# Holding GpSimd's scatter of the normalised rows until the last token tile of the second shared pass is reloaded

## The reference

```python
# first sublayer: x1 = x + tanh(g_xattn) * scan_block(ctx, layernorm(x))
# second sublayer: out = x1 + tanh(g_ffn) * ffn(layernorm(x1))
x = hidden_states.reshape(-1, H)                       # 2048 x 512
scores = softmax(einsum('th,eh->te', x, gate_w))
topk_w, topk_idx = top_k(scores, 2)
combine = sum(one_hot(topk_idx, 16) * topk_w[..., None], axis=1)
gu = einsum('th,ehj->etj', x, w_gate_up)               # 16 x 2048 x 704
h = swiglu(gu, 352)
y = einsum('eti,eih,te->th', h, w_down, combine)
y = y + swiglu(x @ shared_gate_up, 704) @ shared_down
```

## Time and profile before

| | us |
|---|---|
| median of 3 runs | 1187.91 |
| lowest and highest | 1187.38, 1188.02 |
| span of the profiled execution | 1213.6 |
| TensorE matmul busy | 990.7 (82%) |
| VectorE busy | 831.8 (69%) |
| ScalarE busy | 560.9 (46%) |
| GpSimd busy | 538.4 (44%) |

### The profile page before, as it was taken

One profiled execution on the slowest core, in us unless ns is written; L12 is line 12 of the kernel. 1 busy time (PEld: TensorE's weight loads), 2 busy tenths in 40 slices (PEclk: granted clock), 3 DMA queues, 4 the chain that ended last, 5 costly groups with the idle time before them and its releaser, 6 DMA issues.

```text
span 1213.6 us, 21853 instructions
## 1 busy us (share of the span) xinstructions
PE 990.7 (82%) x4756; PEld 720.0 (59%) x4765; DVE 831.8 (69%) x1185; ACT 560.9 (46%) x946; POOL 538.4 (44%) x466
## 2 busy tenths in 40 slices
PE   4568977699778897799779998289999999984687
PEld 2144434444344443455479997278898889883576
DVE  4579899898998989999954446154454545444457
ACT  1485875458655685588232122033443544442211
POOL 0056656466555665599611003702433444441164
PEclk9669999899899999999989999689999999996689
DMA  2314111041012300311031013724556665654367
GB/s 76 120 38 174 36 27 50 21 173 36 25 45 89 111 27 26 106 42 46 18 106 43 35 53 111 272 94 138 178 193 212 214 227 203 204 198 135 106 208 233
DMA packets 66229, 134.93 MB, mean 111 GB/s; under 512 B 9344, under 2 KB 13952, under 8 KB 66176
## 3 DMA queue, kind: packets, MB, share of 16 engines
q1 hardware_dynamic: 56496, 103.64, 26.2%
q0 software_dynamic: 8960, 29.37, 6.8%
q10 hardware_dynamic: 720, 1.31, 0.4%
HBM read 161.43 MB, written 42.07 MB: 168 GB/s over the span
## 4 chain that ended last, share of the span: by engine, by line
PE 52%; DVE 21%; issue 15%; ACT 4%; another core or an unknown queue 3%; DVEq 2%; SPq 1%; POOL 1%; ACTq 0%; DMA 0%; POOLq 0%
PE psY L821 12%; PE psG L785 11%; PE psU L785 10%; PE y_ps L689 6%; DVE hst L1280 6%; PE dbu_ps L676 5%; PE psT L778 3%; DVE by_parity L1232 2%; PE psHT L799 2%; DVE sp_t L1266 2%; ACT dA L994 2%; PE mp L643 1%; DVE y L1263 1%; DVE by_parity L1228 1%
## 5 line engine op out<-in xcount | busy, mean ns | idle before, releaser
L509 POOL TENSOR_TENSOR prod<-hst,cbc 128x512 f32<-128x512 f32 x256 | 343.1, 1351 | 249.5 <-DVE hst L1280 242.1
L1280 DVE TENSOR_TENSOR_SCAN hst<-dA,dbu_ps 128x512 f32<-128x512 f32 x256 | 304.8, 1207 | 29.5 <-PE dbu_ps L676 17.9
L689 PE MATMUL y_ps<-prod,ident 128*128 128x512 f32 x512 | 270.0, 610 | 0.9 <-issue 0.4
L676 PEld LDWEIGHTS dbu_ps<-ident,dbuT 128*128 128x128 f32 x1024 | 123.6, 146 | 225.0 <-DVE hst L1280 161.7
L994 ACT ACTIVATE dA<-by_parity,Aneg 128x512 f32 (+1 forms) x256 | 177.6, 715 | 165.6 <-DVE hst L1280 137.8
L676 PE MATMUL dbu_ps<-ident,dbuT 128*128 128x128 f32 x1024 | 166.7, 287 | 74.0 <-DVE hst L1280 69.4
L1094 ACT CAST hh<-psHT 128x384 fp32r<-128x384 f32 x79 | 37.7, 478 | 318.4 <-PE psHT L799 278.8
L821 PE MATMUL psY<-weights,hh 128*128 (+3 forms) x420 | 138.7, 412 | 32.1 <-DVE hl L1475 24.0
L785 PE MATMUL psG<-weights,xh 128*128 (+1 forms) x560 | 141.2, 335 | 14.5 <-issue 9.9
L785 PE MATMUL psU<-weights,xh 128*128 (+2 forms) x560 | 143.0, 337 | 3.7 <-issue 3.7
L1005 ACT ACTIVATE dbuT<-by_parity,BT 128x512 f32 (+1 forms) x192 | 123.7, 707 | 3.3 <-PE dbu_ps L676 3.3
(11 more groups left out here) (176 smaller groups left out, 1358.5 us busy)
## 6 DMA issues: line engine op xcount, KB each, us to landing
raw_gu<-in_L_ffn_w_gate_up_dram SPq DMA_DIRECT2D x100, 704.0 KB
raw_d<-in_L_ffn_w_down_dram SPq DMA_DIRECT2D x50, 512.0 KB
cbc<-c_rows SPq DMA_DIRECT2D x64, 256.0 KB, 3.2
slot_in<-ztile SPq DMA_DIRECT2D x3, 4096.0 KB, 13.7
gbuf<-slot_in SPq DMA_DIRECT2D x48, 256.0 KB, 3.1
slot_out<-yout POOLq DMA_DIRECT2D x48, 256.0 KB, 3.3
raw_d<-in_L_ffn_w_down_dram SPq DMA_DIRECT2D x50, 192.0 KB
xn_rows<-xin SPq DMA_DIRECT2D x16, 256.0 KB, 2.0
```

The lines of the kernel that those rows point to most:

```text
L509: pool.tensor_tensor(prod[:, slot_of(n, j), :], hst[:, slot_of(n, j), :], cbc[:, n % 2, :], ALU.mult).then_inc(prod_ready, 1)
L676: last = tr(dbu_ps[j % 2][:, t * P:(t + 1) * P], dbuT[:, n % 2, t, j * P:(j + 1) * P], ident[:])
L689: mm(y_ps[j][:], ident[:], prod[:, slot_of(n, j), :], start=False, stop=False).then_inc(prod_used, 1)
L1280: V.tensor_tensor_scan(hst[:, slot_of(n, j), :], dA[:, slot_of(n, j), :], dbu_ps[j % 2][:], 0.0, ALU.mult, ALU.add).then_inc(scanned, 1)
```

## The change

One more wait stands on GpSimd's queue ahead of the first indirect DMA of the scatter. Its count is 16 * (8 // 2) = 64, that is the fourth landing in xin's odd buffer since the pass began: tiles 1, 3, 5 and 7. No other instruction is added, removed or moved.

```diff
@@ -541,6 +541,7 @@
             pool.wait_ge(xn_kept, NT)
             pool.wait_ge(pos_ready, 1)
             pool.wait_ge(zeroed, 16 * (NB - 1))
+            pool.wait_ge(xin_ready[1], 16 * (NB1 // 2))
             for t in range(NT):
                 for c in range(2):
                     pool.indirect_dma_start(
```

## The result

| | before | changed |
|---|---|---|
| median, us | 1187.97 | 1210.82 |
| ratio, 95% interval | | 1.0191 (1.0173 to 1.0209) |
| span of the profiled execution | 1213.6 | 1208.4 |
| TensorE matmul busy | 990.7 | 988.5 |
| GpSimd busy | 538.4 | 538.4 |

The 1210.82 us are the median of four executions, of which one took 5352.13 us and isn't in the ratio; the other three lie between 1210.05 and 1210.92 us.

What follows compares the result with a forecast made beforehand. The prediction took the scatter's end, 4.3 us after the shared pass, to bound the first routed slot. It summed 1187.9 + 18.3 (later scatter) + 0.9 (clock) = 1207.1 us, range 1193 to 1212.

Steps and rivals of the forecast that it cites:

- The hole: TensorE's idle stretch in the second shared pass, empty in 780 to 790 us; claimed not caused by token-tile reloads.
- The scatter ends last: Before the first routed transposes: scattered data ready at 791.5 us, shared pass done at 787.2, so the scatter binds by 4.3.
- The shift: Scatter start moves from 745.0 to 763.3 us, after tile 7 lands; 18.3 us later, passed on in full.
- The split: VectorE splitting the first expert's weights beside the scatter; delays descriptors by 0, at worst +5.2 us in one kernel.
- The rule of the Trainium skill: DMAs of all engines share 16 DMA engines, so holding the scatter frees reloads; if they held slots up, 1178 us.
- The clock: TensorE's cold restart at the first routed products after longer idling: 0 to 1.9 us more, 0.9 taken.
- I take the freeze as something of the profiled execution: Engines' stall during the scatter belongs to the 1213.6 us profiled run, not the 1187.91 us median.
- the rebuilt span: First trace's span without the stall, transposes 28.1 us earlier: 1185.5 us, leaving 2.4 us to the median.
- (a): Stall during the scatter is real and the held-back scatter escapes it: transposes at 809.8, -9.8 us, 1178 us; chance 0.12.
- (b): Stall during the scatter is real and comes back: -6.9 to +14.8 us, likely +8, 1196 us; chance 0.10.

Runs made afterwards that it cites:

- free chips: Two of the four chips, where the unchanged kernel before took 1188.5 and 1188.7 us; the engines did not stall during the scatter.
- the doses: Changed kernel with the scatter waiting for tile 5, tile 6, or tile 7 with first expert's loads also held: ratios 1.0055, 1.0097, 1.0164 to the kernel before.
- freezing one: One of two chips where the unchanged kernel before took 1213.3 and 1212.5 us and engines stalled during the scatter; the change measured 0.9991 on one.
- the unfrozen trace: Kernel before, unchanged, profiled once more on a chip without the stalls: 1187.49 us, ratio 0.9989, span 1188.1 us.

## Why the prediction was right, and where not

**The hole isn't the reloads: right.** No slot of any trace waited for xin.

**The scatter ends last before the change: right on free chips.** By 3.6 us, where 4.3 were worked out; the doses count in full. In the changed kernel the wait is 26.8 us, where 22.6 were worked out: 3.4 us of the difference are the later end of the scatter, 1.5 that TensorE came to this wait sooner, counted from slot NT+1's psG (after 49.2 us instead of 50.7), less the 0.7 that it was shorter before. What made it sooner was not tried.

**The shift: the mechanism right, one term too small.** Tile 7's load was issued at 759.59, as worked out (759.8). Its landing was put at 2.6 us, with 4.0 at most, from the stores of xn_rows and the gbuf loads; it took 5.66. I had written down myself that the first expert's loads stand ahead of the wait and "stay", and didn't see that without the freeze they are issued at 759, together with tile 7: in the trace of before they stood at 762.99 and tile 7 at 790.76, both put off by the freeze. The sum, with measured terms: 21.4 us of later start (18.3 forecast; the other 3.1 are the landing), 0.3 us of slower pace of the scatter, 0.6 us of clock, 22.3 in all, against 22.85 measured and an interval of some 20.6 to 24.8. The split, for which up to 5.2 us were allowed, is in the 0.3: it lengthened three issues by 0.95 us here and three by 0.56 us in the kernel before.

**The rule of the Trainium skill** (DMA: Bandwidth & Descriptors, Issuing engines are not separate DMA queues), that the transfers of all issuing engines interleave on the same 16 DMA engines, was set aside because the rows showed no reload held up. It came back on the other side: the trace agrees with it, 5.66 us beside the expert's 2 MB and 2.66 without them. It spoke for a gain and made part of the loss.

**The clock: 0.9 us forecast, 0.6 measured.** A 3.60 us pause had already brought the clock down: it is 0.50 in 792.5 to 795 of the unfrozen trace, and the first group took 3.70 us, as the row after the 4.45 us pause had said. What the longer pause added is that the clock stayed down longer after it: 11.87 instead of 11.28 us to the second routed slot's psG. The middle of 0 to 1.9 was a choice between the two and not derived; it came out near.

**"I take the freeze as something of the profiled execution": wrong.** This is the step that failed, though the forecast didn't fall with it. That the rebuilt span fits the median was a good argument that the runs behind the 1187.9 us had no freeze, and it agrees with all that was seen on free chips. It didn't show that profiling makes it. The freeze goes with the chip, or with what else differed between the sets of runs: on two chips every execution of the kernel before lay between 1207.8 and 1221.1 us, on two others between 1184.1 and 1191.7, and profiles of the second kind show no freeze. The first trace (1213.6 us) fits the first kind and the first times (1187.9 us) the second, so they most likely came from different conditions; that it was two chips is inferred, not shown. The forecast holds for free chips; on a freezing one the right answer was 0. That the change was measured where the kernel before takes 1188 us was luck: on a chip that behaves as the first trace does, the forecast of a slower kernel would have missed.

**Rivals (a) and (b)**, written for a real freeze, gave -9.8 us and -6.9 to +14.8. On the freezing chip the transposes started at 813.74, where (a) said 809.8 and (b) 812.7 at best: a freeze that comes back and lets work through, which is (b) near its best case. Against 819.57 in the first trace that is 5.8 us sooner, but the times differ by 0.6 us only. Neither the -9.8 nor the -6.9 has in it that the changed kernel restarts cold there. In the first trace TensorE came to these transposes from work:

```profile
828.87 1.92 PE psG L785 x12
```

From 819.57 to this psG are 9.30 us; in the changed kernel it is 11.59 us (813.74 to 825.33), which takes 2.3 us back. For the rest, the kernel before varies there from run to run by 9 us, and the one trace of it that was read stood at the upper part: an execution with a span of 1213.6 us took 1215.2, with a median of 1212.5.

**What stays open.** What on the freezing chips stops the taking up of instructions while an indirect scatter to DRAM runs. It goes with the scatter's time and shows on TensorE, VectorE and ScalarE but not on GpSimd; SyncE's issue of the expert's first loads took 2.13 us in the first trace instead of 0.98. Whether the instructions themselves reach the engines late was not tried; the first trace has no packet on its two queues of kind "instruction" between 750 and 795. Nor was the kernel before, as it is, profiled once more on a freezing chip, or any chip used a second time. Whether those chips would freeze with no recording of a trace at all, no run here could tell, since each execution has its span recorded.

## What to carry to other kernels

A long queue of work that is hidden under another stage may have no slack at all: rebuild the stage without its stalls, see which of the two ends last, and if it is the queue, every microsecond of a later start is paid in full. When a span is longer than the time of the runs, the trace and the times may come from different conditions; profile the kernel once more before reading the trace, and compare the two on one chip. And when a stall is taken out of a trace on paper, move the transfers that it had put off as well: what then falls together is where the estimate is weakest.

## What the runs showed of the hardware

- 32 indirect DMAs from SBUF to DRAM, 256 KB each, take GpSimd 40.4 to 41.4 us from the first start to the last, mostly at a step of 1.27 us, on all chips alike. On two of the four chips (one set of runs on each) TensorE, VectorE and ScalarE stand still for up to 16 us at a time meanwhile, and in the first trace ScalarE for 33; the kernel takes 1213 us there and 1188 on the others. Half as many of them give back 19 us.
- Issues of an indirect DMA that fell beside two-input operations of VectorE in SBUF took longer. In the changed kernel three issues in a row took 1.47, 1.29 and 1.10 us instead of 0.97, beside 5.2 us of splitting (777.65 to 782.73); on the second freezing chip, where the splitting ran from 784.13 to 789.22, the long ones were those at 785.18, 786.96 and 788.56:

```profile
777.90 1.47 POOL L547 DMA_INDIRECT slot_in<-xn_kept_rows,posi  x1 [0.30 <-issue]
779.67 1.29 POOL L547 DMA_INDIRECT slot_in<-xn_kept_rows,posi  x1 [0.30 <-issue]
781.27 1.10 POOL L547 DMA_INDIRECT slot_in<-xn_kept_rows,posi  x1 [0.30 <-issue]
```

  That is 0.95 us in all, far less than the 5.2 us that were allowed for.
- A 256 KB load lands in 2.66 us alone and in 5.66 us (5.86 on the second freezing chip) when the first of 2 MB of loads were issued 0.6 us ahead of it on another queue.
- What a pause of TensorE costs afterwards: to the second slot's psG 9.30 us without a pause, 11.28 after 3.60 us of it, 11.87 after 26.8.
